# A deformable convolution with its input loads merged and moved behind the weight reads, its input sums moved, and its norm cut in four

## The chip, the cores and the metric

The kernel runs on one core of a Trainium2 chip. The metric is the device time in microseconds (us) of one execution; 3 runs were made of the kernel before. Engines: PE is TensorE, DVE is VectorE, ACT is ScalarE, POOL is GpSimd; SPq and ACTq are the DMA queues that SyncE and ScalarE issue to.

## The reference

The input `x` is 32 samples of 64 channels of 56 x 56. Two layers are added to it in turn:

```python
x = x + _L0_conv_ref(_gn(x), ...)   # binarised grouped convolutions with batch norms
x = x + _L1_conv_ref(_gn(x), ...)   # deformable convolution, 8 groups, 9 taps
```

The second is what the change is in. `_gn` is a group norm with 32 groups of two channels. Then:

```python
value = xf @ vp_w.T + vp_b                    # 64 -> 64 channels
om_in = depthwise_3x3(x, dw_w) + dw_b
om = om_in @ om_w.T + om_b                    # per pixel: 8 groups x 9 taps x (2 offsets, 1 mask)
# every tap reads value at its own fractional place, bilinearly, with zeros outside
sampled = gather(y0, x0) * (1-ty)*(1-tx) + ... # four neighbours
out = einsum('nhwgk,nhwgkc->nhwgc', mask, sampled) @ op_w.T
```

All is float32.

## The kernel before

`program` runs `l0_passes` (first layer), then `l1_pass` (second layer), then `general_pass`, which does nothing unless an offset is too far for `l1_pass`. The first layer leaves `x`'s sum with it unfinished: `l1_pass` has still to add three parts, the input `x`, a tensor `x3_d` and a scaled tensor `l2_d` (32 of 64 channels per sample).

`l1_pass` (line 671) works on pairs of samples: 64 channels of one in partitions 0 to 63, of the other in 64 to 127. A pair has NT = 14 blocks of four image rows (TN = 224 pixels), one block in each step. There are 16 pairs: the first is written out, pairs 1 to 14 are a loop on every engine (`Fori`), the last is written out again. All engines run the same sequence of steps `j` = 0 to 13, each with work for a different block, so that the stages form a pipeline. `near(i, j, n, ...)` gives the block `n` steps further on. In step `j`:

- ScalarE: `hats(j+2)` (bilinear hat functions of the offsets, L1089 to L1094), `copy_acc(j-2)` (L1119), `copy_weights(j)` (the window sums from PSUM to `wst`, L1102), `write_weights(j)` (`wst` to DRAM, 400 KB, L1113), in step 9 `normalise` of the whole next pair (L1070), and `taps(j+5)`, the nine depthwise products (L1079).
- GpSimd: `depthwise(j+4)`, four additions of the nine products (L1024 to L1031), then `merge(j+1)`, two additions on `pr` (L1038, L1041), in step 8 `deviation` for the next norm.
- VectorE: `copy_om(j+2)` (offsets and masks out of PSUM, L936), `mask_hats(j+1)`, `products(j+1)` (L945, L955), `read_misc` for the step: the output addition of block `j-2` into `y` (L962) and the value rows of block `j+4` out of PSUM (L928). Behind it, in steps 1, 2, 3 and 5, `sum_piece` of the next pair: two sums over 784 columns (L894, L897) and the statistics (L903).
- TensorE: `apply(j-2)` (the banded weights `abuf` times the value rows `vbd`, L1245), `windows(j)` (L1224), then in `offsets_and_misc` values (L1161), offsets (L1166) and the projection of block `j-2` (L1173).
- SyncE: `read_values(j+2)` (four DMAs, L854), `write_values(j+3)` (L843), in steps 0, 1, 2 and 4 `load_piece` of the next pair (L812 to L815), `read_weights(j)` (seven DMAs of 120 KB from DRAM into `abuf`, L836), which waits for `write_weights(j)`, and in steps 6, 9, 13 and 2 `store_piece` (L823).

A pair's input comes in four pieces of 784 columns. `y` has a buffer for two pairs; `x3h` and `l2h` have two buffers of one piece, so that a load waits for the sum before last (`y_ok`). The semaphore `xl_in` tells VectorE that a piece is in. `misc_ok` tells TensorE that `read_misc` is through: it does not write the next values before. `xp_ok` tells that the normalised image `xp` is there, for `taps` and for the value rows.

## Time and profile before

| | us |
|---|---|
| median of 3 runs | 3491.53 (3486.46 to 3496.63) |
| the profiled execution, its own time | 3484.53 |
| its span | 3482.5 |
| TensorE matmul busy | 2797.9 (80%) |
| TensorE weight load busy | 2290.3 (66%) |
| ScalarE busy | 2010.5 (58%) |
| VectorE busy | 1877.5 (54%) |
| GpSimd busy | 1791.0 (51%) |
| q1 (SyncE's DMA queue) | 54.3% of 16 engines |

Shares are of the whole span; the first layer is in them. The second layer begins with the loads at 905 us. The 224 output additions, one per step, are a clock for it: the first is at 991, the last at 3427 us. A row of a timeline gives start, duration, engine, line, operation, destination<-source, and in brackets how long the engine stood before it and for whom.

### The profile page before, as it was taken

The numbers are of one execution on the slowest core, as the hardware profiler recorded it, in microseconds if no ns is written. First come the engines' busy times: TensorE is split into PE (matmuls) and PEld (weight loads), VectorE is DVE, ScalarE is ACT, GpSimd is POOL, SyncE is SP. The second block draws the span as 40 slices with busy tenths as digits, with TensorE's granted clock in tenths as the row PEclk, the third lists the DMA queues.
The fourth block names the chain that finished last, engine by engine and source line by source line (L and its number), as shares of the span: only waits on it lengthen the run. The fifth ranks groups of instructions, "written<-read, shape, count | busy, mean of one in ns | idle before, by whom it ended". The sixth has DMA issues, their size and how long they took to land. (4 is left out here: it accounts for less than half of the span.)

```text
span 3482.5 us, 117965 instructions
## 1 busy us (share of the span) xinstructions
PE 2797.9 (80%) x47624; PEld 2290.3 (66%) x47624; DVE 1877.5 (54%) x2922; ACT 2010.5 (58%) x4273; POOL 1791.0 (51%) x1450
## 2 busy tenths in 40 slices
PE   4888567778179989897988889798988989798993
PEld 2555345656167777776777777677767777677882
DVE  3554412211476656666565666666565666666651
ACT  1222123222278777676767767686767767676870
POOL 0000000000378677676767677676766777676860
PEclk9999879889589999999999999999999999999996
DMA  4555388886466666666576666657576666657662
GB/s 108 149 143 144 84 203 208 213 206 175 107 158 175 189 177 178 181 171 182 161 190 171 185 180 172 181 165 187 159 189 172 183 181 170 183 163 190 171 171 73
DMA packets 480109, 587.20 MB, mean 169 GB/s; under 512 B 178840, under 2 KB 424032, under 8 KB 479584
## 3 DMA queue, kind: packets, MB, share of 16 engines
q1 hardware_dynamic: 361312, 488.15, 54.3%
q10 hardware_dynamic: 118272, 91.76, 8.3%
q8 instruction: 364, 5.96, 0.7%
q14 instruction: 161, 1.32, 0.1%
HBM read 351.92 MB, written 201.14 MB: 159 GB/s over the span
## 5 line engine op out<-in xcount | busy, mean ns | idle before, releaser
L1245 PE MATMUL acc_p<-abuf,vbd 128*32 128x102 f32 (+7 forms) x27648 | 1091.8, 333 | 297.4 <-DMA abuf<-weight_scratch 219.5
L1245 PEld LDWEIGHTS acc_p<-abuf,vbd 128*32 128x32 f32 (+1 forms) x27648 | 919.0, 145 | 471.6 <-DMA abuf<-weight_scratch 161.7
L1079 ACT ACTIVATE dwt<-xp,wts 128x224 f32<-128x224 f32 x2016 | 798.8, 481 | 140.8 <-ACT wst L1102 102.5
L1024 POOL TENSOR_TENSOR dwt<-dwt 128x896 f32<-128x896 f32 x224 | 496.3, 2216 | 575.3 <-ACT dwt L1079 573.8
L164 PE MATMUL cv<-cin,wb 128*64 128x392 bf16 x6912 | 635.7, 348 | 147.3 <-DMA cin<-sg 147.3
L955 DVE TENSOR_TENSOR pr<-mh_p,ht 128x864 f32<-128x864 f32 x672 | 669.2, 1051 | 23.2
L164 PEld LDWEIGHTS cv<-cin,wb 128*64 128x64 bf16 x6912 | 443.4, 115 | 333.5 <-issue 95.9
L1224 PE MATMUL win_p<-pr,smat 128*128 128x160 f32 x4032 | 610.8, 306 | 12.6 <-POOL pr L1041 12.6
L1224 PEld LDWEIGHTS win_p<-pr,smat 128*128 128x128 f32 x4032 | 556.7, 191 | 33.2 <-POOL pr L1041 10.9
L962 DVE TENSOR_TENSOR y<-y,misc 128x224 f32 (+1 forms) x224 | 86.7, 387 | 833.2 <-PE misc L1173 833.2
L1166 PE MATMUL om_p<-wts,omin 64*64 64x216 f32 x3584 | 378.1, 350 | 6.3 <-POOL omin L1031 6.3
L1102 ACT ACTIVATE wst<-win_p 128x480 f32<-128x480 f32 x448 | 205.1, 513 | 262.9 <-PE win_p L1224 262.8
L1041 POOL TENSOR_TENSOR pr<-pr 128x576 f32<-128x576 f32 x224 | 330.9, 1477 | 31.2
L1038 POOL TENSOR_TENSOR pr<-pr 128x576 f32<-128x576 f32 x224 | 316.7, 1414 | 32.6 <-DVE pr L955 32.6
L171 ACT ACTIVATE lt<-cv 128x392 f32<-128x392 f32 x128 | 60.7, 494 | 447.7 <-PE cv L164 447.7
L1026 POOL TENSOR_TENSOR dwt<-dwt 128x448 f32<-128x448 f32 x224 | 301.9, 1348 | 17.6
L945 DVE TENSOR_TENSOR mh_p<-oms,ht 128x864 f32<-128x864 f32 x224 | 263.2, 1175 | 8.5 <-ACT ht L1094 8.5
L1166 PEld LDWEIGHTS om_p<-wts,omin 64*64 64x64 f32 x3584 | 232.9, 133 | 38.1 <-issue 7.6
L1089 ACT ACTIVATE ht<-oms 128x576 f32<-128x576 f32 x224 | 151.7, 677 | 163.7 <-DVE oms L936 158.3
L936 DVE TENSOR_TENSOR oms<-om_p,ombt 128x864 f32<-128x864 f32 x224 | 235.6, 1052 | 6.3 <-PE om_p L1166 6.3
L666 POOL TENSOR_SCALAR sc<-sc 128x1 f32<-128x1 f32 x1 | 0.2, 222 | 463.1 <-DVE sc L648 463.1
L340 POOL TENSOR_TENSOR gs<-gs,eps 128x2 f32<-128x2 f32 x16 | 3.1, 195 | 356.3 <-DVE gs L299 356.3
(137 smaller groups left out, 2584.0 us busy)
## 6 DMA issues: line engine op xcount, KB each, us to landing
abuf<-weight_scratch SPq DMA_DIRECT2D x1568, 120.0 KB, 2.7
weight_scratch<-wst ACTq DMA_DIRECT2D x224, 400.0 KB, 3.4
xt<-x SPq DMA_DIRECT2D x128, 392.0 KB, 8.3
rows_scratch<-vsb SPq DMA_DIRECT2D x224, 128.0 KB, 2.6
vbd<-rows_scratch SPq DMA_DIRECT2D x896, 32.0 KB, 2.4
cin<-sg SPq DMA_DIRECT2D x128, 203.0 KB, 3.5
x_scratch<-xt SPq DMA_DIRECT2D x64, 392.0 KB, 5.5
y<-x SPq DMA_DIRECT2D x128, 196.0 KB, 3.6
```

Source lines behind the costliest of these rows:

```text
L164: mm = pe.matmul(cv[c][64 * h:64 * h + 64, 0:CN], wb[:, layer, j, k, :], cin[:, u, r:r + CR, k % 3:k % 3 + W], start=(k == 0 and j == 0), ...
L936: dve.tensor_tensor(oms[:, j % 2, :, :].rearrange("q w (k g) -> q w k g", g=G), om_p[:, :].rearrange("q (k z) -> q k z", k=BR)[:, :, 0:OMC ...
L945: dve.tensor_tensor(mh[:, :, :, :], oms[:, j % 2, 2 * TAPS:3 * TAPS, :].unsqueeze(1).broadcast_to([LANES, 3, TAPS, BR * G]), ht[:, j % 2, ...
L955: dve.tensor_tensor(pr[:, j % 2, slots, :, :, :].rearrange("p k e x z -> p e k (x z)"), mh[:, a, :, :].rearrange("p (k x) z -> p k (x z)", ...
L1024: pool.tensor_tensor(d[:, 0:4, :], d[:, 0:4, :], d[:, 4:8, :], ALU.add).then_inc(dw1_ok, 1)
L1026: pool.tensor_tensor(d[:, 0:2, :], d[:, 0:2, :], d[:, 2:4, :], ALU.add).then_inc(dw2_ok, 1)
L1038: pool.tensor_tensor(rows(slice(1, 3)), rows(slice(1, 3)), rows(slice(5, 11, 5)), ALU.add).then_inc(mg1_ok, 1)
L1041: pool.tensor_tensor(rows(slice(2, 4)), rows(slice(2, 4)), rows(slice(8, 5, -2)), ALU.add).then_inc(mg_ok, 1)
L1079: ins = act.activation(dwt[:, j % 2, k, :].rearrange("p (r w) -> p r w", w=W), image[:, r:r + BR, k % 3:k % 3 + W], ACT.Identity, scale=dw ...
L1166: return pe.matmul(om_p[64 * s:64 * s + 64, 256 * r:256 * r + OMC], omin[64 * s:64 * s + 64, j % 2, r, :], omw[64 * s:64 * s + 64, :], sta ...
L1224: mm = pe.matmul(win_p[:, to:to + 160], smat[:, e, :], pr[:, j % 2, 0:RT, a, b, :].rearrange("p r (k g) -> p k r g", g=G), start=n == 0, s ...
L1245: mm = pe.matmul(acc_p[32 * (2 * s + b):32 * (2 * s + b) + 32, 0:TN].rearrange("p (k w) -> p k w", w=W)[:, k0:k1 + 1, x0:x1], vbd[0:K, 1 - ...
```

## The change

- SyncE: `load_piece` stands behind `read_weights` and `store_piece` in its step, and not ahead of them. The loads of `y` and of `x3h` are one DMA of 128 partitions each in place of two of 64; the two of `l2h` stay. So a piece has four DMAs and not six. A piece's store is one DMA and not two. Pieces 2 and 3 are loaded in steps 3 and 5 (2 and 4 before).
- VectorE: `sum_piece` and `channel_stats` stand ahead of `read_misc` in their step; pieces 2 and 3 are summed in steps 4 and 6 (3 and 5 before).
- GpSimd: `merge` stands ahead of `depthwise`.
- ScalarE: the norm is done in four parts of 14 rows. Each is issued at the beginning of the first `taps` that needs it: in steps 9 and 12 and, in the next pair, 1 and 5. It waits no longer for `misc_ready`. `taps` and the value rows wait for the parts that they need.

```diff
-        LOAD_AT = (0, 1, 2, 4)
-        SUM_AT = (1, 2, 3, 5)
-        STATS_AT, GROUPS_AT, NORM_AT = 7, 8, 9
+        LOAD_AT = (0, 1, 3, 5)
+        SUM_AT = (1, 2, 4, 6)
+        STATS_AT, GROUPS_AT = 7, 8
+        NORM_ROWS = H // 4
...
+        def norm_needed(j):
+
+            return min(H - 1, BR * (j + 1)) // NORM_ROWS
...
+                    sp.dma_start(y[:, bass.ts(q % 2, 1), at].rearrange("p a f -> p (a f)"),
+                                 x.rearrange("(q s) c f -> q (s c) f", s=S)[bass.ts(q, 1), :, at].rearrange("a p f -> (a p) f")).then_inc(xl_in[k % 2], 16)
+                    sp.dma_start(x3h[:, k % 2, :],
+                                 x3_d.rearrange("(q s) c f -> q (s c) f", s=S)[bass.ts(q, 1), :, at].rearrange("a p f -> (a p) f")).then_inc(xl_in[k % 2], 16)
                     for s in range(S):
-                        sp.dma_start(y[64 * s:64 * s + 64, bass.ts(q % 2, 1), at].rearrange("p a f -> p (a f)"),
-                                     x[S * q + s, :, at]).then_inc(xl_in[k % 2], 16)
-                        sp.dma_start(x3h[64 * s:64 * s + 64, k % 2, :], x3_d[S * q + s, :, at]).then_inc(xl_in[k % 2], 16)
                         sp.dma_start(l2h[64 * s:64 * s + CO, k % 2, :],
...
-                    for s in range(S):
-                        sp.dma_start(out[S * q + s, :, at],
-                                     y[64 * s:64 * s + 64, bass.ts(q % 2, 1), at].rearrange("p a f -> p (a f)")).then_inc(out_ok[k], 16)
+                    sp.dma_start(out.rearrange("(q s) c f -> q (s c) f", s=S)[bass.ts(q, 1), :, at].rearrange("a p f -> (a p) f"),
+                                 y[:, bass.ts(q % 2, 1), at].rearrange("p a f -> p (a f)")).then_inc(out_ok[k], 16)
...
-                    if not last and j in LOAD_AT:
-                        load_piece(i + 1, LOAD_AT.index(j))
                     read_weights(i, j)
                     if j in STORE_AT:
                         back, k = STORE_AT[j]
                         if not (first and back):
                             store_piece(i - back, k)
+                    if not last and j in LOAD_AT:
+                        load_piece(i + 1, LOAD_AT.index(j))
...
-                    read_misc(phase(i, j), i + 1 if j == GROUPS_AT and not last else None,
-                              near(i, j, 4, first, last), near(i, j, -2, first, last))
                     if not last:
                         if j in SUM_AT:
                             sum_piece(i + 1, SUM_AT.index(j))
                         if j == STATS_AT:
                             channel_stats(i + 1)
+                    read_misc(phase(i, j), i + 1 if j == GROUPS_AT and not last else None,
+                              near(i, j, 4, first, last), near(i, j, -2, first, last))
...
+                    n = near(i, j, 1, first, last)
+                    if n:
+                        merge(*n)
                     n = near(i, j, 4, first, last)
                     if n:
                         depthwise(*n)
-                    n = near(i, j, 1, first, last)
-                    if n:
-                        merge(*n)
...
-                def normalise(q):
+                def normalise(q, m):
+
                     act.wait_ge(nb3_ok, q + 1)
-                    wait(act, misc_ready, phase(q, 0) - 4)
-                    act.activation(image[:, 1:1 + H, 1:1 + W],
-                                   y[:, bass.ts(q % 2, 1), :].rearrange("p a (r w) -> p (a r) w", w=W),
+                    rows = slice(NORM_ROWS * m, NORM_ROWS * (m + 1))
+                    act.activation(image[:, 1 + NORM_ROWS * m:1 + NORM_ROWS * (m + 1), 1:1 + W],
+                                   y[:, bass.ts(q % 2, 1), :].rearrange("p a (r w) -> p (a r) w", w=W)[:, rows, :],
                                    ACT.Identity, scale=g3[:, 2:3], bias=g3[:, 3:4]).then_inc(xp_ok, 1)
 
                 def taps(i, j):
+                    for m in range(4):
+                        if norm_needed(j) == m and (j == 0 or norm_needed(j - 1) < m):
+                            normalise(i, m)
                     wait(act, dw_ok, NT * i + j - 1)
-                    act.wait_ge(xp_ok, i + 1)
+                    act.wait_ge(xp_ok, 4 * i + norm_needed(j) + 1)
...
-                    if not last and j == NORM_AT:
-                        normalise(i + 1)
...
                     if value:
-                        pe.wait_ge(xp_ok, value[0] + 1)
+                        pe.wait_ge(xp_ok, 4 * value[0] + norm_needed(value[1]) + 1)
```

## Rows read from the trace of the kernel before

**Rows 1.** Waits of the whole run: engine line waited for: us, times, longest.
```profile
DVE y L962 <- PE misc L1173: 833.2, 209, 11.2
...
PE acc_p L1245 <- DMA abuf<-weight_scratch: 219.5, 73, 7.3
```

**Rows 2.** Timeline of an undisturbed step: start us, duration us, engine and operation.
```profile
2323.30 0.38 ACTq L1113 DMA_DIRECT2D weight_scratch<-wst  x1
...
2324.24 0.39 DVE L962 TENSOR_TENSOR y<-y,misc 128x224 f32 x1 [3.37 <-PE misc L1173]
...
2325.06 1.06 DVE L936 TENSOR_TENSOR oms<-om_p,ombt 128x864 f32<-128x864 f32 x1
...
2326.28 3.59 SPq L836 DMA_DIRECT2D abuf<-weight_scratch  x7
```

**Rows 3.** Timeline of two steps with a load.
```profile
2202.80 0.43 ACTq L1113 DMA_DIRECT2D weight_scratch<-wst  x1
...
2203.99 0.39 DVE L962 TENSOR_TENSOR y<-y,misc 128x224 f32 x1 [10.65 <-PE misc L1173]
...
2204.97 1.56 SPq L843 DMA_DIRECT2D rows_scratch<-vsb  x1
...
2207.64 0.61 SPq L812 DMA_DIRECT2D y<-x  x1
...
2212.40 3.52 SPq L836 DMA_DIRECT2D abuf<-weight_scratch  x7
2212.85 0.39 DVE L962 TENSOR_TENSOR y<-y,misc 128x224 f32 x1 [2.95 <-PE misc L1173]
...
2220.05 4.22 PE L1245 MATMUL acc_p<-abuf,vbd 128*32 128x102 f32 x96 [7.34 <-DMA abuf<-weight_scratch]
...
2229.16 0.39 DVE L962 TENSOR_TENSOR y<-y,misc 128x224 f32 x1 [3.61 <-PE misc L1173]
```

**Rows 4.** The same timeline: the sum, and the hats behind it.
```profile
2216.25 2.72 DVE L897 SCALAR_TENSOR_TENSOR y<-l2h,ab,y 128x784 f32 x1
...
2220.02 1.04 DVE L936 TENSOR_TENSOR oms<-om_p,ombt 128x864 f32<-128x864 f32 x1
...
2221.15 0.69 ACT L1089 ACTIVATE ht<-oms 128x576 f32<-128x576 f32 x1 [5.31 <-DVE oms L936]
...
2224.40 0.36 ACT L1119 ACTIVATE accs<-acc_p 128x224 f32<-128x224 f32 x1
```

**Rows 5.** VectorE's timeline, the output addition of step 7 of that pair.
```profile
2284.31 0.39 DVE L962 TENSOR_TENSOR y<-y,misc 128x224 f32 x1 [3.64 <-PE misc L1173]
```

**Rows 6.** Timeline of the step with the norm.
```profile
2303.79 0.39 DVE L962 TENSOR_TENSOR y<-y,misc 128x224 f32 x1 [3.27 <-PE misc L1173]
...
2303.82 3.05 ACT L1070 ACTIVATE xp<-y,g 128x3136 f32 x1 [1.22 <-PE misc L1173]
...
2313.48 0.33 ACT L1119 ACTIVATE accs<-acc_p 128x224 f32<-128x224 f32 x1
...
2314.66 0.39 DVE L962 TENSOR_TENSOR y<-y,misc 128x224 f32 x1 [4.93 <-PE misc L1173]
```

**Rows 7.** Windows: stretch, its us, five engines' busy, PEclk, DMA share, GB/s.
```profile
434.40:435.90 1.50, 0.00 (x0) 0.00 (x0) 0.00 (x0) 0.00 (x0) 0.00 (x0) 0.50 1.00 401
...
917.50:921.00 3.50, 0.00 (x0) 0.00 (x0) 2.21 (x5) 0.00 (x0) 0.00 (x0) 0.50 0.96 214
```

**Rows 8.** Timelines of the first layer and of the loads ahead of the steps.
```profile
430.34 0.58 SPq L504 DMA_DIRECT2D lin<-l_scratch  x1
...
905.08 0.53 SPq L812 DMA_DIRECT2D y<-x  x1
...
911.98 1.04 DVE L894 SCALAR_TENSOR_TENSOR y<-y,ab,x3h 128x784 f32<-128x784 f32 x1 [12.83 <-DMA l2h<-l_scratch]
...
914.19 1.02 DVE L903 BATCH_NORM_STATS2 bn<-y 128x6 f32<-128x392 f32 x2
```

**Rows 9.** Instructions on `lin`: duration ns min/median/max, first and last start.
```profile
L504 SPq DMA_DIRECT2D lin<-l_scratch x16: 584/1224/1566, 427.1 to 832.4; - x16
```

## What the change is predicted to do

> **What bounds the kernel now.** First the waits, longest in total [rows 1]. The largest wait that TensorE has on anything outside itself is for `abuf`, the weight bands read back from DRAM: 219.5 us in 73 waits. 15 of the 16 pairs of samples load the next pair's input, which makes 14.6 us per pair. VectorE, in contrast, stands 833.2 us before its output addition waiting for TensorE: that is the idle time into which the change puts the input sums.
>
> Then the timeline of one undisturbed step [rows 2]. Output additions are 9.58 us apart (2314.66 [rows 6] to 2324.24), which is TensorE's own work. Taking one addition (2324.24) as zero: ScalarE issued the band write at -0.94, SyncE began the seven reads at +2.04, 2.98 after the write was issued, and took 3.6 to issue them. VectorE began the next step at +0.82.
>
> Then a load step [rows 3]. The band write goes out at 2202.80; by the same 2.98 us it could be read at 2205.8, and SyncE is free at 2206.53 (2204.97 + 1.56). But first come six load DMAs from 2207.64, and the weight reads start at 2212.40. TensorE stands 7.34 us and applies them at 2220.05. The outputs at 2212.85 and 2229.16 are 16.3 apart instead of about 9. The other loads do the same: from 2203.99 to the seventh output after it at 2284.31 [rows 5] are 80.3 us.
>
> **The change part by part.**
> *Weight reads ahead of the loads.* In this pair they would start at about 2206.9 and be issued by 2210.3 (3.4 for seven, between the 3.2 and 3.6 of the timeline). Their data is there some 2.5 later, at 2212.8, when TensorE wants it (the output before is at 2212.85). This wait goes. What is late next is the load itself, since the sums now stand before VectorE's output addition and before the next `copy_om`, and not behind the addition.
>
> *The new chain.* Load lands, sum, addition and value copy, `copy_om` (L936), hats (L1089 to L1094), `copy_acc` (L1119), projection, output. Its pieces: 0.2 to see the semaphore; a sum alone takes 3.2 (911.98 to 914.19 + 1.02 [rows 8]); addition to `copy_om` 0.82 [rows 2]; `copy_om` to hats 1.13 and hats to `copy_acc` 3.25 [rows 4]; `copy_acc` to the output addition 1.18 (2313.48 to 2314.66 [rows 6]). Together 9.8 us from landing to output. So the wait that the change adds is VectorE's wait for `xl_in`. Behind it in VectorE's queue stand the addition of this step, the values, and `copy_om` and the products of the next; on `copy_om` wait the hats, and behind the hats in ScalarE's queue stand `copy_acc`, for which TensorE's projection waits, and the copy and write of the next bands. The trace of before shows the link: the hats waited 5.31 on `copy_om` after the sum [rows 4], at no cost then, as TensorE stood for the weights anyway.
>
> *When the load lands.* Before, six transfers of 64 or 32 partitions: first issue to landing 6.9 us on an otherwise idle queue (905.08 to 911.98 [rows 8]), at 214 GB/s with the DMA engines 96% busy [rows 7]: bound by the transfer, not by the issue. Merged, `x` and `x_3` are 128-partition transfers. The trace has one large read of that kind, `lin` in the first layer, issued at 430.34 [rows 8] behind other reads: while it moves, from 434.4 on, the engines carry 401 GB/s, and are as busy as at 214 [rows 7]. So 2 x 392 KB at 401 take 2.0 us and the two `l_2` transfers of 98 KB, still 32 partitions each, take 0.9 at 214: 3 us instead of 4.7 for all at 214. They queue behind the weight reads, whose data ends about 2.2 after their last issue; then 3.0, and about 0.6 for the band write of 400 KB that comes along and shares the engines (alone it is 1.9 at 214 GB/s; it meets only the end of the load). Landing 5.8 us after the last weight read is issued. Bounds: 5.2 if the band write costs nothing, 8.5 if merging speeds nothing up and most of the band write lies inside it (2.2 + 4.7 + 1.6).
>
> The Trainium skill says the same of the partitions (SBUF — State Buffer, "Door 1: The DMA port swizzle"): 64 partitions reach 8 of 16 ports, as 32 do, and only 128 reach all. By that the trace agrees, 214 against 401 GB/s; by its asymptote of 436 GB/s the two merged transfers would take, as an estimate, 1.8 us and not 2.0.
>
> *The sum.* With the load settled the five outputs follow. In this pair:
> - output 0: weight reads issued by 2210.3, landing 2216.1, output 2225.9 (was 2229.16);
> - output 1: the second load lands before VectorE has finished its products, so TensorE's 9.58 decides, plus 0.8 for a slower sum: 2236.3;
> - output 2: 2245.9, no load and no sum (pieces 2 and 3 moved one step);
> - output 3: band write at 2235.2, readable 2238.2, issued 2241.5, landing 2247.3, plus 9.8 and 0.3 contention: 2257.4 (TensorE alone would be at 2255.5);
> - output 4: 2267.0;
> - output 5: the band write follows the late `copy_acc` at 2257.5, readable 2260.6, issued 2263.9, landing 2269.7: 2279.8 (was 2284.31; TensorE alone 2276.6).
> 4.5 us per pair of the 14.6 are gained; the rest becomes the wait for the landing.
>
> *The sum beside GpSimd.* The second instruction of a sum took 2.72 instead of 1.03 in the load step [rows 4]; in the new place most sums find GpSimd done, since they wait for the data until it is. I take 0.3 per sum and 0.8 for piece 1, whose data is there early; the row's 1.7 each is the upper end, nothing the lower. The Trainium skill speaks against the move here (SBUF — State Buffer, "Who interferes with whom"): a VectorE instruction with two SBUF inputs and a GpSimd instruction that reads SBUF exclude each other for the whole instruction. Our row of 2.72 fits it. By that rule a sum that comes just behind the start of GpSimd's first depthwise addition (2216 ns in the page's group of L1024) would lose about 2.2 us; four such per pair would take the gain of 4.5 away.
>
> *The norm in four.* ScalarE's norm, 3.05 us and a wait of 1.22 ahead of it, made `copy_acc` late and that output interval 10.87 (2303.79 to 2314.66) instead of 9.58 [rows 6]: 1.3 per pair. So 3.0 of the 4.3 us were absorbed by ScalarE's slack. A quarter is about 0.9 (3.05 / 4 and a little for the fixed part) and its wait is gone: it fits, and all 1.3 goes. The other quarters come before the taps of steps 12, 1 and 5, under the same slack or under the load's wait; if it were gone there, 0.9 each. The normalised image is read in quarters by `value_row`, four steps ahead at least.
>
> *Merge ahead of the depthwise additions.* TensorE's windows hardly ever waited for the merge (it is not among the long waits), so this is worth nothing alone. It lets late products reach TensorE in time, as four depthwise additions (4.9 us) no longer stand between. The price is that they now stand behind VectorE: where VectorE is held by the sum, so are they, but the offsets that read them come one step later. I take nothing; up to 0.5 per load step if that cover is gone.
>
> *Stores merged.* One DMA fewer in four steps where SyncE was not late: nothing.
>
> *Before the first step.* Four loads in a row with sums between: 1.5 less for the first, about 1 less for the others, 2.1 less norm, part of it hidden: 5 us.
>
> 15 x (4.5 + 1.3) + 5 = 92 us. The profiled run took 3484.5, the median of the runs is 7 more. 3484.5 - 92 = 3392.5; as a median 3400 us.
>
> **The rivals.** One microsecond of landing time costs about 3 us per pair (outputs 0, 3 and 5), 45 in all.
> - *Slower: VectorE blocks on the load.* If merged transfers run at 214 GB/s like the old ones, the load lands at 8.5; that is 2.7 later than forecast and 8.1 per pair, against 4.5 + 1.3 gained: 2.3 per pair slower than before, 35 in all: 3525 us. Merely losing the gain takes a landing at 7.7. For it: the load is the last in the queue now and the sum wants it 4 us earlier. Against: the 401 GB/s.
> - *No change: the long issue.* The `lin` read took SyncE between 0.58 and 1.57 to issue [rows 9], as the queue was empty or full. With two such a load takes 4.0 to issue and not 2.4; it lands 0.8 later and SyncE comes late to the next weight read (3.4 + 4.0 + 2.7 + 0.5 and gaps exceed 9.58), 2.3 more. 1.1 per pair is left: 3475.
> - *Faster still: the landing hides.* It would have to come 3.8 after the last weight read, before the data can be through. Then the whole 14.6 + 1.3 goes: 3250. Half way, with no contention at all and a landing at 5.2, 3340.
>
> **How the numbers follow.** Forecast with its spread of landing times (5.2 to 6.8, 3340 to 3450) 0.65; the long issue 0.12; blocking 0.13; hiding 0.10. Range 3330 to 3485: it takes in the long issue and leaves out blocking and full hiding. 0.3% is 10 us, about what a measurement of this kernel can tell from no change. Faster by more than that 0.81 (forecast, hiding, half of the long issue), within it 0.06 (the other half), slower 0.13.
>
> **What would show it.** Right: TensorE's wait for `abuf` falls from 219.5 to under 60; VectorE's wait for `l2h` in L894 rises from nearly nothing to over 100; hats wait for `copy_om` longer; GB/s in load steps near 400 while the merged transfers move; the normal interval 9.58 unchanged and the one at the norm down from 10.87 to 9.58. Wrong: no wait at L894 (hiding), or load packets at the old rate (blocking), or weight reads that start over 3 us behind the end of their write (long issue).

## The result and the profile after

| | before | after |
|---|---|---|
| median, us | 3493.45 | 3573.78 |
| profiled execution, span | 3482.5 | 3569.0 |
| output additions, first and last | 991, 3427 | 995, 3514 |

The ratio is 1.0227, with a 95% interval of 1.0202 to 1.0251: slower by 80 us, where 92 us faster were forecast. The loss lies in the steps. The mean time of one pair, from projection to projection, was 155.3 us in pairs 1 to 14 and is 161.2.

The waits of the kernel after, in the columns of [rows 1]:

```profile
POOL pr L1043 <- DVE pr L960: 646.9, 155, 11.6
DVE y L967 <- PE misc L1179: 483.7, 135, 10.8
...
DVE y L899 <- DMA l2h<-l_scratch: 422.9, 60, 12.2
ACT ht L1098 <- DVE oms L941: 390.2, 63, 9.2
...
PE misc L1167 <- DVE oms L941: 152.4, 54, 4.5
...
PEld acc_p L1251 <- DMA abuf<-weight_scratch: 51.9, 53, 4.0
```

TensorE's wait for the weights is gone, as forecast. In its place VectorE stands 422.9 us before the input sum for the load to land (about 27 us per pair, after the 12 of the first load of all), and the hats stand 390.2 us for `copy_om` behind it.

The timeline of pair 8 of the kernel after, steps 0 to 2, answers to [rows 3]:

```profile
2247.66 0.41 ACTq L1122 DMA_DIRECT2D weight_scratch<-wst  x1
...
2252.92 3.87 SPq L841 DMA_DIRECT2D abuf<-weight_scratch  x7
...
2257.40 0.38 SPq L816 DMA_DIRECT2D y<-x  x1
...
2259.13 4.24 PE L1251 MATMUL acc_p<-abuf,vbd 128*32 128x102 f32 x96 [1.56 <-DMA abuf<-weight_scratch]
...
2263.88 1.03 DVE L899 SCALAR_TENSOR_TENSOR y<-y,ab,x3h 128x784 f32 x1 [9.12 <-DMA l2h<-l_scratch]
2264.95 1.03 DVE L902 SCALAR_TENSOR_TENSOR y<-l2h,ab,y 128x784 f32 x1
...
2266.09 1.02 DVE L908 BATCH_NORM_STATS2 bn<-y 128x6 f32 x2
2267.03 0.37 DVE L967 TENSOR_TENSOR y<-y,misc 128x224 f32 x1
...
2267.76 1.05 DVE L941 TENSOR_TENSOR oms<-om_p,ombt 128x864 f32<-128x864 f32 x1
...
2268.90 0.68 ACT L1098 ACTIVATE ht<-oms 128x576 f32<-128x576 f32 x1 [6.79 <-DVE oms L941]
...
2271.97 0.33 ACT L1128 ACTIVATE accs<-acc_p 128x224 f32<-128x224 f32 x1
...
2272.40 0.60 PE L1179 MATMUL misc<-accs,wts 64*64 64x112 f32 x8 [0.18 <-issue]
```

The whole chain of the prediction can be read off: the weights cost TensorE 1.56 us in place of 7.34, then VectorE stands 9.12 for the load, sums, adds the output that TensorE had finished long before, and only then makes the offsets on which hats, `copy_acc` and projection stand in a row.

The merged transfers do run faster. Windows while the input load moves, kernel after (columns as in [rows 7]): the loads issued at 2257.40, 2293.35 and 2267.72.

```profile
2259.40:2262.90 3.50, 3.50 (x80) 3.04 (x76) 0.00 (x0) 2.71 (x7) 2.05 (x3) 1.00 0.92 305
2295.50:2298.90 3.40, 3.40 (x76) 2.59 (x72) 0.00 (x0) 1.58 (x4) 3.10 (x4) 1.00 1.00 324
2269.80:2272.00 2.20, 2.20 (x22) 1.24 (x14) 2.12 (x3) 2.20 (x6) 0.02 (x1) 0.50 1.00 390
```

390 GB/s in the best window and 305 to 324 in the two longer ones, in which the 32-partition transfers of `l2h` and other traffic lie too, against 208 in the kernel before while its load moved:

```profile
2209.00:2213.00 4.00, 3.71 (x52) 2.90 (x50) 1.05 (x2) 2.92 (x7) 3.70 (x5) 1.00 0.90 208
```

### The profile page after: what moved, and what is told of

It reads as the page before. It is cut to its first block and busy times, and to the rows that moved or that the text cites. A ratio compares the mean times of both kernels' runs of the same rounds, so it can differ in the third digit from the quotient of the medians.

```text
span 3569.0 us, 117609 instructions
## 1 busy us (share of the span) xinstructions
PE 2853.7 (80%) x47624; PEld 2306.5 (65%) x47624; DVE 1929.4 (54%) x2922; ACT 2023.2 (57%) x4321; POOL 1836.2 (51%) x1450
## 5 line engine op out<-in xcount | busy, mean ns | idle before, releaser
L1251 PEld LDWEIGHTS acc_p<-abuf,vbd 128*32 128x32 f32 (+1 forms) x27648 | 905.7, 145 | 319.3 <-issue 102.5
L1043 POOL TENSOR_TENSOR pr<-pr 128x576 f32<-128x576 f32 x224 | 316.8, 1414 | 646.9 <-DVE pr L960 646.9
L1172 PE MATMUL om_p<-wts,omin 64*64 64x216 f32 x3584 | 414.3, 375 | 2.4 <-issue 2.4
L1098 ACT ACTIVATE ht<-oms 128x576 f32<-128x576 f32 x224 | 151.8, 677 | 395.9 <-DVE oms L941 390.2
L1046 POOL TENSOR_TENSOR pr<-pr 128x576 f32<-128x576 f32 x224 | 321.9, 1437 | 31.3
L1167 PE MATMUL misc<-wts,xp 64*64 64x64 f32 x3584 | 184.2, 239 | 183.2 <-DVE oms L941 152.4
L950 DVE TENSOR_TENSOR mh_p<-oms,ht 128x864 f32<-128x864 f32 x224 | 309.3, 1381 | 2.5 <-ACT ht L1103 2.5
L899 DVE SCALAR_TENSOR_TENSOR y<-y,ab,x3h 128x784 f32 (+1 forms) x64 | 74.8, 1168 | 423.1 <-DMA l2h<-l_scratch 422.9
L1167 PEld LDWEIGHTS misc<-wts,xp 64*64 64x64 f32 x3584 | 150.4, 141 | 225.0 <-issue 225.0
L1172 PEld LDWEIGHTS om_p<-wts,omin 64*64 64x64 f32 x3584 | 248.3, 142 | 43.6 <-issue 3.9
```

The lines of the kernel that those rows point to most:

```text
L950: dve.tensor_tensor(mh[:, :, :, :], oms[:, j % 2, 2 * TAPS:3 * TAPS, :].unsqueeze(1).broadcast_to([LANES, 3, TAPS, BR * G]), ht[:, j % 2, ...
L1043: pool.tensor_tensor(rows(slice(1, 3)), rows(slice(1, 3)), rows(slice(5, 11, 5)), ALU.add).then_inc(mg1_ok, 1)
L1046: pool.tensor_tensor(rows(slice(2, 4)), rows(slice(2, 4)), rows(slice(8, 5, -2)), ALU.add).then_inc(mg_ok, 1)
L1167: return pe.matmul(misc[64 - 64 * s:128 - 64 * s, to:to + C], xp[64 * s:64 * s + 64, at:at + XL], vpw[64 * s:64 * s + 64, :], start=True, ...
L1172: return pe.matmul(om_p[64 * s:64 * s + 64, 256 * r:256 * r + OMC], omin[64 * s:64 * s + 64, j % 2, r, :], omw[64 * s:64 * s + 64, :], sta ...
L1251: mm = pe.matmul(acc_p[32 * (2 * s + b):32 * (2 * s + b) + 32, 0:TN].rearrange("p (k w) -> p k w", w=W)[:, k0:k1 + 1, x0:x1], vbd[0:K, 1 - ...
```

## The experiments

The theory at this point: one cause, VectorE blocked on a load that lands too late for the place of the sum, passed on by `copy_om`, hats and `copy_acc`. The rivals: GpSimd's new order, the quarter norms on ScalarE, the merged transfers, SyncE's queue.

| kernel | median, us | ratio to before (95%) |
|---|---|---|
| before | 3493 to 3496 | 1 |
| changed kernel | 3573.8 | 1.0227 (1.0202 to 1.0251) |
| changed, sums one step later | 3330.9 | 0.9511 (0.9483 to 0.9538) |
| changed, sums behind the addition | 3541.8 | 1.0112 (1.0077 to 1.0147) |
| before, transfers merged only | 3382.0 | 0.9661 (0.9627 to 0.9695) |
| before, sums ahead only | 3492.7 | 0.9992 (0.9972 to 1.0012) |
| before, loads behind only | 3608.2 | 1.0315 (1.0297 to 1.0334) |
| before, norm in four only | 3471.6 | 0.9934 (0.9920 to 0.9948) |
| changed, GpSimd's old order | 3602.1 | 1.0300 (1.0280 to 1.0320) |
| changed, loads ahead again | 3379.1 | 0.9682 (0.9658 to 0.9706) |
| sums later, GpSimd's old order | 3321.4 | 0.9505 (0.9476 to 0.9534) |
| changed, `l2h` not loaded | 3502.3 | 1.0027 (1.0013 to 1.0042) |
| sums later, part of `x` apart | 3399.9 | 0.9726 (0.9696 to 0.9755) |
| sums later, six transfers | 3409.9 | 0.9761 (0.9728 to 0.9794) |

### Sums one step later

```diff
-        SUM_AT = (1, 2, 4, 6)
+        SUM_AT = (2, 3, 5, 7)
```

> The changed kernel with each input sum one step later (steps 2, 3, 5 and 7 in place of 1, 2, 4 and 6), nothing else. Theory (VectorE blocks on a load that has not landed: the load lands about 7.3 us after the last weight read is issued, and the sum wants it 5 us earlier): the wait for the load ahead of the sum, 422.9 us in the changed kernel, falls below 40 us, and the kernel to about 3325 us, below the one before. Rival 1 (GpSimd's new order makes the depthwise additions late) and rival 2 (the quarter norms stand in ScalarE's way): about 3570, as the changed kernel. Rival 3 (SyncE, with the load in its queue, comes late to the next weight read, and TensorE waits for that): the wait for the load goes, but TensorE's wait for the weights is back at 150 us or more and the time is above 3450.

3330.9 us: one line turns 80 us lost into 163 gained. Its waits:

```profile
PE acc_p L1251 <- DMA abuf<-weight_scratch: 81.9, 76, 3.8
...
ACT ht L1098 <- DVE oms L941: 34.2, 26, 3.0
...
DVE y L899 <- DMA l2h<-l_scratch: 19.6, 12, 11.9
```

The wait for the load is down to 19.6 us, 11.9 of which are the first load of all, and the hats' to 34.2. GpSimd's order, the quarter norms, the merging and SyncE's order are all in this kernel, so none of them alone is what made the changed one slow.

### Sums behind the addition again

```diff
+                    read_misc(phase(i, j), i + 1 if j == GROUPS_AT and not last else None,
+                              near(i, j, 4, first, last), near(i, j, -2, first, last))
                     if not last:
                         if j in SUM_AT:
                             sum_piece(i + 1, SUM_AT.index(j))
                         if j == STATS_AT:
                             channel_stats(i + 1)
-                    read_misc(phase(i, j), i + 1 if j == GROUPS_AT and not last else None,
-                              near(i, j, 4, first, last), near(i, j, -2, first, last))
```

> The changed kernel with the input sums behind the output addition again, at the same steps 1, 2, 4 and 6: VectorE's part of the change undone alone. Theory: VectorE still has to wait for the landing before the next copy_om, only without the addition and value copy behind it, and about 4 us of its wait are spent on the addition first; the chain from landing to output is 0.8 us shorter and TensorE's values no longer wait: 3 us per pair better than the changed kernel, about 3530 us, still slower than before. Rival (it is the place of the sum ahead of the addition alone that costs): near 3400. Rivals 1 and 2 of the run before: 3570.

3541.8, 32 us better than the changed kernel and still slower than before. The wait ahead of the sum is smaller, as part of it passes in the wait for the addition, but the hats' wait is nearly as long:

```profile
ACT ht L1098 <- DVE oms L941: 374.3, 78, 9.1
...
DVE y L899 <- DMA l2h<-l_scratch: 237.3, 56, 11.7
```

So it is not the place against the addition that decides but that the next `copy_om` is queued behind a wait for the load.

### The parts alone

Merged transfers on the kernel before (the merging lines of the change's diff, the stores' too, with the counts of their semaphores; the places of loads and sums as before):

```diff
+                    sp.dma_start(x3h[:, k % 2, :],
+                                 x3_d.rearrange("(q s) c f -> q (s c) f", s=S)[bass.ts(q, 1), :, at].rearrange("a p f -> (a p) f")).then_inc(xl_in[k % 2], 16)
                     for s in range(S):
-                        sp.dma_start(x3h[64 * s:64 * s + 64, k % 2, :], x3_d[S * q + s, :, at]).then_inc(xl_in[k % 2], 16)
...
-                    dve.wait_ge(xl_in[k % 2], 6 * 16 * (PIECES // 2 * q + k // 2 + 1))
+                    dve.wait_ge(xl_in[k % 2], 4 * 16 * (PIECES // 2 * q + k // 2 + 1))
```

> The kernel before with the loads and the stores merged into 128-partition transfers and nothing else: loads stay ahead of the weight reads, sums where they were. Theory: the load is issued in 2.2 us and not 4.3, the weight reads start 2 us earlier in the four load steps and their wait on TensorE shrinks by 6 to 7 us per pair: 3400 us, and the packets of the merged transfers take about 130 ns in place of 204. Rival (the merging is what costs, since larger transfers hold the queue longer): 3490 or more.

3382.0: 114 us faster, somewhat more than expected. TensorE's wait for the weights fell from 219.5 to 115.8 us.

Sums ahead of the addition, on the kernel before:

```diff
-                    read_misc(phase(i, j), i + 1 if j == GROUPS_AT and not last else None,
-                              near(i, j, 4, first, last), near(i, j, -2, first, last))
                     if not last:
                         if j in SUM_AT:
                             sum_piece(i + 1, SUM_AT.index(j))
                         if j == STATS_AT:
                             channel_stats(i + 1)
+                    read_misc(phase(i, j), i + 1 if j == GROUPS_AT and not last else None,
+                              near(i, j, 4, first, last), near(i, j, -2, first, last))
```

> The kernel before with only the sums (and the channel statistics) moved ahead of the output addition, at their old steps 1, 2, 3 and 5. Theory: the loads are issued ahead of the weight reads and land 4 us earlier than in the changed kernel, so VectorE waits 2 to 3 us per sum, inside the time that TensorE stands for the weights anyway: within 10 us of before, 3490. Rival (the move of the sum alone costs, wherever the load is): 3540 or more.

3492.7, a ratio of 0.9992: nothing, as expected. VectorE's wait for the load rose to 188.4 us and cost nothing, as TensorE was waiting for the weights meanwhile (235.3).

Loads behind the weight reads, on the kernel before:

```diff
-                    if not last and j in LOAD_AT:
-                        load_piece(i + 1, LOAD_AT.index(j))
                     read_weights(i, j)
...
+                    if not last and j in LOAD_AT:
+                        load_piece(i + 1, LOAD_AT.index(j))
```

> The kernel before with only the loads moved behind the weight reads (still six transfers a piece, steps 0, 1, 2 and 4, sums behind the output addition). Theory: TensorE's wait for the weights goes, but the load lands about 8 us after the last weight read is issued, 3 us later than VectorE wants it, and the chain from the landing over copy_om and the hats gives the gain back: 3490, within 25 us of before, with a wait for the load ahead of the sums of over 150 us. Rival (the reads' place alone is what counts): 3300 to 3380.

3608.2: 112 us slower, where no change was expected. The direction of the theory held and its size did not. TensorE's wait for the weights fell to 28.2, and there came 312.2 us before the sum and 433.0 before the hats. The piece loaded in step 2 stands behind the weight reads and a store as well; the timeline of pair 8:

```profile
2319.91 1.47 SPq L823 DMA_DIRECT2D out<-y  x2
2321.84 0.53 SPq L812 DMA_DIRECT2D y<-x  x1
...
2331.00 1.03 DVE L894 SCALAR_TENSOR_TENSOR y<-y,ab,x3h 128x784 f32 x1 [7.96 <-DMA l2h<-l_scratch]
...
2334.15 1.04 DVE L936 TENSOR_TENSOR oms<-om_p,ombt 128x864 f32<-128x864 f32 x1
...
2335.29 0.68 ACT L1089 ACTIVATE ht<-oms 128x576 f32<-128x576 f32 x1 [9.10 <-DVE oms L936]
...
2339.55 0.39 DVE L962 TENSOR_TENSOR y<-y,misc 128x224 f32 x1 [0.29 <-PE misc L1173]
```

9.2 us from the first transfer of the load (2321.84) to the sum, and 8.6 more to the output (2339.55). Over pairs 1 to 13 the sums of the four pieces started 9.1, 7.5, 11.5 and 9.3 us after the last weight read was issued, where the landing had been put at 8; that is the part of the size that the expectation had wrong.

The norm in four parts, on the kernel before:

```diff
-                    act.wait_ge(xp_ok, i + 1)
+                    for m in range(4):
+                        if norm_needed(j) == m and (j == 0 or norm_needed(j - 1) < m):
+                            normalise(i, m)
...
+                    act.wait_ge(xp_ok, 4 * i + norm_needed(j) + 1)
...
-                    if not last and j == NORM_AT:
-                        normalise(i + 1)
...
-                normalise(0)
```

> The kernel before with only the norm in four parts. Theory: the output interval at the norm falls from 10.9 to 9.6 us in 15 pairs, 20 us, and the beginning of the second layer loses 4 us, since the values of block 3 wait for the second quarter and the first offsets stand behind them on TensorE: 3478. Rival (the quarters stand in ScalarE's way in steps 1 and 5): 3500 or more.

3471.6, with a ratio of 0.9934: a gain of 23 us. In the profile the interval at the norm fell from 10.88 to 9.58 us on average, the 20 us expected, while the other intervals of a pair were 1.1 us longer in sum; that profile is the slowest execution of its kernel (3479.0) and the one of before is among the fastest of its own (3484.5), so this difference says little; the loss expected at the beginning did not come (its first output addition is at 989.4 us, before at 991.2).

These parts alone sum to -114 + 0 + 112 - 23 = -25 us, and GpSimd's order gave 28 more in the changed kernel (below). The changed kernel is 80 us slower, so the parts don't add. Two reasons can be read off. The sums ahead cost nothing with the loads ahead of the weight reads and 32 us with the loads behind them (3573.8 against 3541.8). And the merging's 114 us came with a shorter wait of TensorE for the weights, which the loads' new place takes away as well: what both take away can be gained once only. How much of the rest that is was not run.

### GpSimd's order

```diff
+                    n = near(i, j, 4, first, last)
+                    if n:
+                        depthwise(*n)
                     n = near(i, j, 1, first, last)
                     if n:
                         merge(*n)
-                    n = near(i, j, 4, first, last)
-                    if n:
-                        depthwise(*n)
```

> The changed kernel with GpSimd's old order, depthwise ahead of merge. Theory: what is late in the blocked steps is VectorE, not GpSimd, so this changes nothing: 3574, within 15 us. Rival (the depthwise additions behind VectorE are what costs): 3520 or less.

3602.1: in the changed kernel the new order is worth 28 us, neither nothing nor a cost. The likely reason is in the sums: with their statistics they take 4.3 us on average with the old order and 3.7 with the new one, and for piece 0 5.0 and 3.3. The timeline with the old order, where depthwise additions are beside the sum:

```profile
2286.36 1.03 DVE L899 SCALAR_TENSOR_TENSOR y<-y,ab,x3h 128x784 f32 x1 [6.78 <-DMA l2h<-l_scratch]
2287.02 2.32 POOL L1029 TENSOR_TENSOR dwt<-dwt 128x896 f32<-128x896 f32 x1 [2.46 <-ACT dwt L1088]
2287.43 2.74 DVE L902 SCALAR_TENSOR_TENSOR y<-l2h,ab,y 128x784 f32 x1
```

2.74 us in place of 1.03. With merge ahead, GpSimd was done with all its work when the load landed.

The same diff on the kernel with the sums one step later:

```diff
-        SUM_AT = (1, 2, 4, 6)
+        SUM_AT = (2, 3, 5, 7)
...
+                    n = near(i, j, 4, first, last)
+                    if n:
+                        depthwise(*n)
                     n = near(i, j, 1, first, last)
```

> The kernel with the sums one step later (the run of 3331), with GpSimd's old order, depthwise ahead of merge. In the changed kernel this order cost 28 us, with sums of 4.9 us in place of 3.2, since merge fell beside them. Theory (the cost is the two engines hindering each other): here the sums are 4.7 us long already with the new order, since they start with the products' end, as merge does; with the old order depthwise is beside them, and little changes: within 15 us of 3331. Rival (merge ahead is worth something by itself, since late products reach TensorE sooner): 3350 or more.

3321.4 against 3330.9, with intervals of the ratio that overlap: no difference shown, as expected. But the ground that the expectation gave does not hold. The groups of all 64 second sum instructions, first the kernel after, then sums later, then sums later with the old order:

```profile
L902 DVE SCALAR_TENSOR_TENSOR y<-l2h,ab,y 128x784 f32 (+1 forms) x64 | 88.4, 1382 | 2.3
```
```profile
L902 DVE SCALAR_TENSOR_TENSOR y<-l2h,ab,y 128x784 f32 (+1 forms) x64 | 130.8, 2044 | 2.3
```
```profile
L902 DVE SCALAR_TENSOR_TENSOR y<-l2h,ab,y 128x784 f32 (+1 forms) x64 | 93.9, 1467 | 2.3
```

The mean goes from 1382 to 2044 ns with the sums later, and back to 1467 with the old order; a whole sum with its statistics takes 4.7 us with the new order there and 4.1 with the old. So merge ahead of depthwise shortens sums that wait for a late load and lengthens sums that don't.

### The load's landing moved

Loads ahead of the weight reads again, the rest as changed:

```diff
+                    if not last and j in LOAD_AT:
+                        load_piece(i + 1, LOAD_AT.index(j))
                     read_weights(i, j)
...
-                    if not last and j in LOAD_AT:
-                        load_piece(i + 1, LOAD_AT.index(j))
```

> The changed kernel with the merged loads ahead of the weight reads again, sums at steps 1, 2, 4 and 6 ahead of the output addition as in the changed kernel. Theory: the load is issued 4 us earlier relative to the weight reads, so it lands 4 us earlier, VectorE's wait halves (below 220 us) and lies inside TensorE's wait for the weights: 3365 us, near the kernel with merging alone less the norm's 20. Rival (the sums ahead of the addition cost whatever the load does): above 3450.

3379.1, with the wait for the load at 77.1. The same sums at the same place cost little when the load is issued some 4 us earlier: merging alone gives 3382, less the norm's 23 is 3359, so some 20 us.

The load made smaller (`l2h` isn't loaded, so the sum lacks that part):

```diff
-                    for s in range(S):
-                        sp.dma_start(l2h[64 * s:64 * s + CO, k % 2, :],
-                                     l2_d[bass.ts(q, 1), CO * s:CO * (s + 1), at].rearrange("a c f -> (a c) f")).then_inc(xl_in[k % 2], 16)
...
-                    dve.wait_ge(xl_in[k % 2], 4 * 16 * (PIECES // 2 * q + k // 2 + 1))
+                    dve.wait_ge(xl_in[k % 2], 2 * 16 * (PIECES // 2 * q + k // 2 + 1))
```

> The changed kernel without the loads of l2h (the sum reads zeros for that part): the load has two transfers and not four, nothing else changes. Theory (the landing of the load sets the time, three times per pair at 1 us per us): two issues of 0.45 and 1 us of transfer less, the load lands 1.3 to 1.9 us earlier and the wait for it ahead of the sums falls by 60 to 85 us; time 3490 to 3515. Rival (the wait is an accident beside another limit): 3560 or more.

3502.3, 71 us less, and the wait ahead of the sum fell from 422.9 to 338.6. The sums start 6.0 us after the last weight read is issued and not 7.5 (mean of pairs 1 to 13), so 4.7 us per pair go with 1.5 us of landing: the slope of about 3 to 1 that the prediction worked with.

### What else the later sums need

Six transfers in place of four, with the sums one step later (the stores stay merged):

```diff
-                    sp.dma_start(x3h[:, k % 2, :],
-                                 x3_d.rearrange("(q s) c f -> q (s c) f", s=S)[bass.ts(q, 1), :, at].rearrange("a p f -> (a p) f")).then_inc(xl_in[k % 2], 16)
                     for s in range(S):
+                        sp.dma_start(x3h[64 * s:64 * s + 64, k % 2, :], x3_d[S * q + s, :, at]).then_inc(xl_in[k % 2], 16)
...
-                    dve.wait_ge(xl_in[k % 2], 4 * 16 * (PIECES // 2 * q + k // 2 + 1))
+                    dve.wait_ge(xl_in[k % 2], 6 * 16 * (PIECES // 2 * q + k // 2 + 1))
```

> The kernel with the sums one step later, and the loads in six transfers again (the stores stay merged). Theory: issue of 4.2 us and not 2.3, so that SyncE comes 2 us later to the next weight read, and the load lands 1.5 us later, which with the later sums just fits: 3 to 4 us per pair, 3385. Rival (with the sums later the merging is worth nothing): 3340 or less.

3409.9, 25 us above the expectation: merging is worth 79 us there, and TensorE's wait for the weights is 158.5 us against 81.9.

Part of `x` apart from the rest of its piece:

```diff
+        Y_AT = (0, 2, 4, 4)
...
+                            if j == Y_AT[k]:
+                                load_y(i + 1, k)
```

> The kernel with the sums one step later, and the part of x of pieces 1, 2 and 3 loaded in steps 2, 4 and 4, apart from the rest of their piece (steps 1, 3 and 5). Theory: what is left there per pair are 1.9 us in the interval behind the two consecutive loads and 0.7 to 0.9 in four others, with band writes of 4 to 5 us in place of 3.2 beside the load's traffic; with less in steps 0, 1, 3 and 5 about 2 us per pair go: 3300. Rival (SyncE's issue and waits are what is left): 3331 or more.

3399.9, 69 us slower than the kernel that it was made from. The expectation overlooked the very rule of this case: the `x` part of piece 1 is now loaded in step 2 for a sum in step 3, one step ahead. Its waits show it:

```profile
DVE y L910 <- DMA y<-x: 186.0, 30, 9.4
ACT ht L1109 <- DVE oms L952: 171.7, 57, 7.7
```

30 waits, two per pair; with pieces 0 and 3 loaded two and three steps ahead, it is pieces 1 and 2 that hold VectorE.

The kernel with the sums one step later beats both: 3331 us, 4.9% faster than before (with GpSimd's old order 3321, not told apart from it).

## Why the prediction was wrong

Two terms were mis-sized: the landing of the load (5.8 us after the last weight read, measured 7.7 in the three loads that count) and the band write with the weight reads ahead of it (6.3 us, measured 8.4 to 8.6). The first alone would have used up the gain; with the second the sign turned.

**What bounds the kernel, and the wait that goes.** Right. The weight wait fell from 219.5 to 51.9 us.

**The new chain.** Right, link by link. It was put at 9.8 us from landing to output, 9.6 of them from the start of the sum. In a later load step of pair 8:

```profile
2283.78 0.37 ACTq L1122 DMA_DIRECT2D weight_scratch<-wst  x1
...
2289.07 3.83 SPq L841 DMA_DIRECT2D abuf<-weight_scratch  x7
...
2293.35 0.38 SPq L816 DMA_DIRECT2D y<-x  x1
...
2300.02 1.03 DVE L899 SCALAR_TENSOR_TENSOR y<-y,ab,x3h 128x784 f32 x1 [8.02 <-DMA l2h<-l_scratch]
...
2309.70 0.39 DVE L967 TENSOR_TENSOR y<-y,misc 128x224 f32 x1 [0.69 <-PE misc L1179]
```

2300.02 to 2309.70 is 9.7.

**The rate of the merged transfers.** Right for the packets: the load's packets of 3136 bytes took 124 ns in the median and had taken about 200 before; 16 engines at 124 ns are 405 GB/s (401 expected). The load as a whole did not move at that rate, for the reason below.

**When the load lands.** This term failed. The last weight read is issued at 2292.90 (2289.07 + 3.83); the sum starts 7.1 us later, not 6.0 (5.8 and the 0.2). Over pairs 1 to 13 the landing was 7.8, 6.1, 7.5 and 8.0 us after it for the four pieces. Piece 1 hardly counts (VectorE waited 0.7 us for it on average); the other three, which make outputs 0, 3 and 5, land 7.7 after it on average. The packets tell which part was short: the load's are the ones of 3136 bytes on q1, the weights' have 1920, the band write's are the 800-byte packets on q10. Means of these three loads in pairs 1 to 13, in us:

| | forecast | measured |
|---|---|---|
| end of the weights' data, after the last weight read | 2.2 | 1.78 |
| from there to the load's first data | 0 | -0.01 |
| the load's own packets, spread over 16 engines | 3.0 | 3.31 |
| packets of the band write in that stretch | 0.6 | 0.90 |
| other packets in it, and engines done before the last one | 0 | 1.16 |
| last data to the sum | 0.2 | 0.75 |
| sum | 6.0 | 7.89 |

So on average the load's data did follow directly on the weights' data, as assumed. What failed was to take the queue for empty but for a part of the band write: the traffic of the value rows, part of it issued right behind the load (0.6 us of the 1.16), and the uneven finish of the engines were put at nothing, and the time from the last data to its semaphore as well. In the step above, which is no average one in this, the band write had the engines for itself for 1 us before the load's data came, and then the load moved at 306 GB/s:

```profile
2294.20:2295.20 1.00, 0.17 (x12) 0.17 (x14) 0.00 (x0) 1.00 (x4) 1.00 (x2) 1.00 1.04 293
2295.20:2299.20 4.00, 4.00 (x102) 3.19 (x101) 0.00 (x0) 1.88 (x5) 3.70 (x4) 1.00 0.97 306
```

Even at the beginning of the second layer, where only the next piece's transfers are behind it on the queue, the merged load takes 6.3 us from issue to sum, and had taken 6.9. It was counted as 3 us of data; but its data comes 1.0 us after the issue, and the engines are then busy for 3.7 us at 296 GB/s before the last part lands:

```profile
904.82 0.35 SPq L816 DMA_DIRECT2D y<-x  x1
...
911.15 1.03 DVE L899 SCALAR_TENSOR_TENSOR y<-y,ab,x3h 128x784 f32<-128x784 f32 x1 [12.24 <-DMA l2h<-l_scratch]
```
```profile
904.80:905.70 0.90, 0.00 (x0) 0.00 (x0) 0.00 (x0) 0.00 (x0) 0.00 (x0) 0.50 0.00 0
905.80:909.50 3.70, 0.00 (x0) 0.00 (x0) 0.00 (x0) 0.00 (x0) 0.00 (x0) 0.50 0.99 296
```

A check was there in [rows 8]: 6.9 us from issue to sum, less 1.7 for the faster data, and 0.4 between weight read and load, is 5.6 without a band write, and 7.5 with the whole 1.9 of it. The forecast of 5.8 stood near the lower end.

**Band write and weight reads ahead of the load.** This term failed as well. They were taken from an undisturbed step ([rows 2]: 3.0 us from write to reads) and 3.3 for issuing the reads. In the step above 5.3 us pass (2283.78 to 2289.07) and the reads take 3.8; on average it is 8.6 us together ahead of the load of step 3 and 8.4 ahead of that of step 5, where 6.3 stood. From band write to sum: forecast 12.3 us, measured 16.2. That difference of 3.9 is what output 3 lost against the forecast: its interval is 15.4 us on average, 11.5 was forecast.

The packets show where the band write is late. In the step above its data moves at 291 GB/s until 2286; then 33 of its 528 packets, one engine's share, trail for over 2 us:

```profile
2284.50:2286.00 1.50, 1.50 (x55) 1.30 (x50) 1.50 (x4) 1.50 (x5) 1.50 (x2) 1.00 0.98 291
2286.50:2288.80 2.30, 2.30 (x60) 1.84 (x56) 2.30 (x1) 2.30 (x6) 2.22 (x2) 1.00 0.07 16
```
```profile
q10 hardware_dynamic: 33, 0.03, 4.9%
```

Beside the first part lies a packet of 16 KB on another queue, q8, whose kind the profile gives as instruction. In pairs 1 to 14 the last tenth of a band write's packets takes 1.5 us on average where such a packet lies beside the rest (59 writes), and 0.6 where none does (135). In steps 2, 3, 5 and 7 one lies beside 49 of 56 writes. That these packets hold up one engine fits all this, and was not tested.

**What it adds up to.** Against the forecast the three landings cost 5.7 us per pair, the band writes and reads of steps 3 and 5 cost 4.3, and output 1 came 1.7 late. Measured over the outputs 0 to 5 the forecast was 11 us per pair short, and steps 8 and 9 took 1.1 more than before: 5.8 gained less about 12 is the 5.9 lost per pair, within the rounding of the parts. The beginning, put at 5 us gained, lost 4 (first output 995.5 and not 991.2).

**The sum beside GpSimd.** The 0.3 for the sums that wait was enough (3.2 us, as alone). For piece 1, whose sum starts with merge and depthwise, the forecast was 4.0 and the measured mean 5.2.

**The norm.** Right: 1.3 us per pair, 23 us alone.

**Merge ahead.** Valued at nothing, worth 28 us in this kernel, most likely by keeping GpSimd out of the sums' way.

**The rivals.** It was the rival named blocking, with 0.13, at 3525; the measured time is 49 us above that. Its place, its chain and its point of decision were right: it lost the whole gain at a landing of 7.7, and 7.7 it was. Its reason was wrong: it was tied to merged transfers that run no faster, so the 401 GB/s seemed to exclude it. It should have been tied to the landing, which has other parts, and its chance set by how near 5.8 was to 7.7, at a slope of 3 us per pair for each. The chances of 0.81 for faster rested on a term with an uncertainty of 2 us and a weight of 45 us each. The long issue did not come (0.4 us for a merged transfer in the rows above); its premise that the `lin` read took 0.58 on an empty queue was a misreading, as both reads of 0.58 stand directly behind four reads of `xt`.

**The signs.** All that were named for a right prediction came: a weight wait under 60 us (51.9), a wait for `l2h` over 100 (422.9), longer waits of the hats (390.2 against 158.3), near 400 GB/s in one window, 9.58 and 9.59 in the quiet intervals. They fit a loss as well as a gain, since the waits that the change adds had a lower bound and no upper one.

## What to carry to other kernels

A load that an in-order engine waits for has to be issued so far ahead that it has landed when the engine comes to it. Moving a load behind other transfers and its consumer forward in the same edit shortens that distance from both sides; here the load's move alone cost 112 us, and the consumer's nothing before it and 32 us on top of it. Count from the issue of the last transfer ahead of it, add every transfer that shares the engines with it and the time from its last data to the semaphore, and add what is queued behind the wait on the consumer, up to the engine that sets the end. Give a wait that a change adds an upper bound too. Here one step more of distance was worth 243 us.

## What the runs showed of the hardware

- The same 980 KB load went from 6.9 to 6.3 us from issue to sum when the two larger parts went from 64 to 128 partitions, with only the next piece behind it on the queue. A packet of 3136 bytes took 124 ns in the median where it had taken about 200. In the busy queue the merging was worth far more: 114 us alone. Two things changed there at once, SyncE's issue (2.3 us in place of 4.3 on average, so that the reads behind start earlier) and the time of the data; the runs do not part them.
- With the queue empty the load's first data came 1.0 us after its issue. In the steps its last data came 0.75 us before the sum started.
- A band write of 400 KB, 528 packets, was through to nine tenths 2.2 us after its issue in steps 2, 3, 5 and 7 of the kernel after, as in the quiet steps; its last packets came at 3.5 to 3.8 us there and at 2.4 to 2.6 in steps 10 and 12.
- A sum on VectorE beside additions on GpSimd took 2.74 us in place of 1.03 in the row shown, and the first depthwise addition beside it 2.32 in place of 2.1. The Trainium skill (SBUF — State Buffer, "Who interferes with whom") says that a VectorE instruction with two inputs in SBUF and a GpSimd instruction that reads SBUF contend for a port that one of them holds alone. The row fits that: the addition ran from 2287.02 to 2289.34, the sum was begun at 2287.43, and 1.03 us counted from the addition's end is 2290.37; it ended at 2290.17.
